# Adds moved behind their projections in VectorE's order, with three other placements, in a four-layer graph network kernel

## What is computed

```python
def L0(x, adj, w):                       # d = (rowsum(adj) + 1) ** -0.5
    return relu((d[:, None] * (adj + eye) * d[None, :]) @ x @ w)
def L1(x, adj, W, b):                    # s = (rowsum(adj) + 1e-8) ** -0.5
    return (s[:, None] * adj * s[None, :]) @ x @ W.T + b
def L2(x, A, W):                         # like L0, with rsqrt
    return relu(A_norm @ x @ W)
def L3(x, adj, ...):                     # attention and a plain aggregation, gated
    h = x @ W_sa
    e = where(adj != 0, exp(-leaky_relu(s_left[:, None] + s_right[None, :], 0.01)), 0)
    x_a = (e / (rowsum(e) + 1e-5)) @ h
    x_b = adj @ (x @ W_gcnb) + b_gcnb
    return sigmoid(attn_a * x_a + attn_b * x_b)
```

## Time and profile before

| | |
|---|---|
| median of 3 runs | 1775.53 us (1772.66 to 1776.35) |
| profiled execution | 1777.48 us, span 1775.7 us |
| TensorE busy | 1701.0 us, 96% of the span |
| VectorE, ScalarE, GpSimd busy | 63%, 44%, 34% |
| chunks by time | 6 begins at 399 us, 24 at 1392 us |

### The profile page before, as it was taken

How to read it: one execution, slowest core, us unless ns; L and a number is a source line. 1 busy time by engine, 2 the same in 40 slices (tenths; PEclk the granted TensorE clock), 3 DMA queues, 4 the chain that set the end, 5 groups by cost and what they waited for, 6 DMA issues and landing times.

```text
span 1775.7 us, 31699 instructions
## 1 busy us (share of the span) xinstructions
PE 1701.0 (96%) x12862; PEld 1164.4 (66%) x12862; DVE 1111.8 (63%) x1957; ACT 773.8 (44%) x1178; POOL 605.2 (34%) x567
## 2 busy tenths in 40 slices
PE   3999999999899998999999999999999999999998
PEld 1444444657786887887887887788788544444445
DVE  5786887967768666533543445553641566787765
ACT  5674655544444443322322223210111568677655
POOL 0001655537646444420321111121200446455441
PEclk9999999999999999999999999999999999999999
DMA  9994688698777879876664879976644443444434
GB/s 392 349 347 149 216 321 314 222 342 288 279 276 270 315 248 329 306 282 215 232 227 139 287 243 316 355 245 233 216 143 161 143 128 99 143 138 116 142 96 133
DMA packets 185559, 417.08 MB, mean 235 GB/s; under 512 B 18340, under 2 KB 79136, under 8 KB 181680
## 3 DMA queue, kind: packets, MB, share of 16 engines
q1 hardware_dynamic: 151544, 337.14, 56.4%
q10 hardware_dynamic: 33868, 77.90, 11.5%
HBM read 303.80 MB, written 111.17 MB: 234 GB/s over the span
## 4 chain that ended last, share of the span: by engine, by line
PE 74%; DVE 12%; DMA 5%; ACT 4%; POOL 2%; issue 2%; SPq 0%; ACTq 0%; DVEq 0%; POOLq 0%
PE ps L1139 15%; PE ps L1185 11%; PE ps L1186 11%; PE ps L1187 11%; PE ps L1232 7%; PE ps L1234 7%; PE ps L1233 7%; DVE U L1484 4%; DMA U<-in_adjT 3%; DVE stage L1467 1%; ACT U L1812 1%; DVE CT L1523 1%; DMA U<-in_adj 1%; ACT U L1735 1%; DVE OT L1530 1%
## 5 line engine op out<-in xcount | busy, mean ns | idle before, releaser
L1185 PE MATMUL ps<-U,HB 128*128 128x256 f16 (+2 forms) x2520 | 634.6, 260 | 8.6 <-DVE U L1484 4.1
L1186 PE MATMUL ps<-U,HB 128*128 128x256 f16 (+2 forms) x2520 | 634.4, 260 | 0.0
L1187 PE MATMUL ps<-U,HB 128*128 128x256 f16 (+2 forms) x2520 | 634.2, 260 | 0.0
L1232 PE MATMUL ps<-U,HB 128*128 128x512 f16 (+3 forms) x960 | 341.5, 359 | 21.4 <-DVE U L1484 14.4
L1233 PE MATMUL ps<-U,HB 128*128 128x512 f16 (+3 forms) x960 | 341.1, 358 | 0.0
L1234 PE MATMUL ps<-U,HB 128*128 128x512 f16 (+3 forms) x960 | 340.7, 358 | 0.0
L1484 DVE SCALAR_TENSOR_TENSOR U<-U,cS 128x512 f16<-128x512 f32 (+6 forms) x255 | 253.8, 1019 | 105.0 <-ACT U L1812 104.1
L1139 PE MATMUL ps<-W,OT 128*128 128x512 f16 (+1 forms) x1320 | 302.9, 384 | 9.9 <-DVE xr L1553 7.5
L1185 PEld LDWEIGHTS ps<-U,HB 128*128 128x128 f16 x2520 | 246.3, 98 | 38.8 <-DVE U L1484 5.2
L1812 ACT ACTIVATE U<-U,cS 128x512 f16<-128x512 f32 (+6 forms) x255 | 198.6, 803 | 159.3 <-POOL U L2006 49.7
L1186 PEld LDWEIGHTS ps<-U,HB 128*128 128x128 f16 x2520 | 246.5, 98 | 26.1
(11 more groups left out here) (207 smaller groups left out, 1884.3 us busy)
## 6 DMA issues: line engine op xcount, KB each, us to landing
U<-Ad SPq DMA_DIRECT2D x83, 896.0 KB, 6.7
U<-in_adjT SPq DMA_DIRECT2D x289, 256.0 KB, 4.4
Ad<-U ACTq DMA_DIRECT2D x35, 896.0 KB, 5.3
xd<-xr SPq DMA_DIRECT2D x84, 256.0 KB, 5.8
xr<-xd SPq DMA_DIRECT2D x84, 256.0 KB, 5.2
U<-in_adj SPq DMA_DIRECT2D x14, 1354.0 KB, 8.7
U<-Ad SPq DMA_DIRECT2D x23, 707.0 KB, 5.0
HBd<-stage ACTq DMA_DIRECT2D x16, 896.0 KB, 9.5
```

Source lines behind the costliest of these rows:

```text
L1185: eng.matmul(o, h[0], hi, start=J == 0 and a == 0, stop=False)
L1186: eng.matmul(o, h[0], lo, start=False, stop=False)
L1187: last = eng.matmul(o, h[1], hi, start=False, stop=to in "acg" and J == 9 and a == 1)
L1232: eng.matmul(o, h[0], hi, start=j == 0, stop=False)
```

## The change

Six edits to the planner; no stage is added or taken out but the merged ones.

1. `post(v, p, t)` in `spaced`: the post of a tile in chunks 6 to 23 stands right behind its `project`, no longer at `max(v + 1, later(v, 1.5))`.
2. `at_us` of chunk 6: layer 0's last four projections are planned at 6.5, 9.5, 12.5, 15.5 us instead of 8, 11.5, 15, 18.5.
3. `FETCH`: the first five adjacency rows of chunk 24 are fetched ahead of rows 18 to 21 of chunk 23. The old loop went by SEQ.
4. `pairs`: in layer 1, for J = 0 and 1, and for J = 2 and 3, spread, root and norms are done once for four tiles, when the second pair is complete.
5. `quiet` behind pair 9 is 6.5 us instead of 8; in layer 1 `xbias` and `x_keep` of pairs 9 and 10 are planned 4 us later.
6. `z_keep` stands 8 us behind its `post` instead of 5.2.

```diff
+_cut = AT["agg", GE - 1, 18]
+FETCH = SEQ[:_cut] + SEQ[_cut + 4:_cut + 9] + SEQ[_cut:_cut + 4] + SEQ[_cut + 9:]
...
-        while fetched < len(SEQ) and (fetched <= u + 9 or near(SEQ[fetched], u, 9, 28 if SEQ[fetched][1] == 12 else 20)):
-            g, j = SEQ[fetched][1:]
+        while fetched < len(SEQ) and (fetched <= u + 9 or near(FETCH[fetched], u, 9, 28 if FETCH[fetched][1] == 12 else 20)):
+            g, j = FETCH[fetched][1:]
...
+    def pairs(u, l, J):
+
+        both = l == 1 and J < 4
+        if both and J % 2 == 0:
+            return
+        J0 = J - 1 if both else J
+        t0, nt = 2 * J0, 2 * (J + 1 - J0)
+        put("spread", l, t0, nt)
+        late = 2.6 if l == 1 and J < 7 else 0
+        if late:
+            plan(max(later(u, late), u + 1), "root", l, t0, nt)
+        else:
+            put("root", l, t0, nt)
+        plan(max(later(u, 2.6 + late), u + 1), "norms", l, t0, nt)
+        for i in range(J0, J + 1):
+            pair(max(later(u, 5.2 + late), u + 2), l, i)
+
     def pair(u, l, J):
         nonlocal quiet
-        late = 2.6 if l == 1 and J < 7 else 0
-        if late:
-            plan(max(later(u, late), u + 1), "root", l, 2 * J, 2)
-        else:
-            put("root", l, 2 * J, 2)
-        plan(max(later(u, 2.6 + late), u + 1), "norms", l, 2 * J, 2)
-        u = max(later(u, 5.2 + late), u + 2, quiet)
+        u = max(u, quiet)
...
         if l == 1:
-            steps += [(5, "xbias", 2 * J), (5, "xbias", 2 * J + 1)]
-        steps += [(9, "x_keep", "post", l - 1, 2 * J), (9, "x_keep", "post", l - 1, 2 * J + 1)]
+            steps += [(5 if J < 9 else 9, "xbias", 2 * J), (5 if J < 9 else 9, "xbias", 2 * J + 1)]
+        steps += [(9 if l > 1 or J < 9 else 13, "x_keep", "post", l - 1, t) for t in (2 * J, 2 * J + 1)]
...
-        quiet = later(u, 8 if J >= 7 else 12)
+        quiet = later(u, 6.5 if J == 9 else 8 if J >= 7 else 12)
...
-            plan(later(v, 5.2), "z_keep", t)
+            plan(later(v, 8), "z_keep", t)
...
-        at_us = {0: (8, 11.5, 15, 18.5), 4: (9, 18), 5: (3, 10, 16.5, 23)}.get(c, (12, 18.5, 25, 31.5))
+        at_us = {0: (6.5, 9.5, 12.5, 15.5) if now == GW else (8, 11.5, 15, 18.5), 4: (9, 18), 5: (3, 10, 16.5, 23)}.get(c, (12, 18.5, 25, 31.5))
...
-            post(max(v + 1, later(v, 1.5)), p, t)
+            post(v, p, t)
...
             if stage[0] == "pair":
-                put("spread", stage[1], 2 * stage[2], 2)
-                pair(u, *stage[1:])
+                pairs(u, *stage[1:])
```

More of the change, by code:

```diff
@@ L344, in fetch_to @@
         while fetched < n:
-            put("fetch", *SEQ[fetched])
+            put("fetch", *FETCH[fetched])
             fetched += 1
```

## The result

The kernel after takes 1782.38 us (median; 1780.27 to 1783.36), the kernel before 1773.17 us in the same comparison: ratio 1.0033, 95% interval 1.0021 to 1.0045. It is slower by 0.33% (the two medians alone lie 0.52% apart; the ratio with its interval is used here). The forecast was 1756.6 us, and its range ended at 1769. The profiled execution of after took 1783.36 us with a span of 1781.5 us, 5.8 us more than before's 1775.7.

A forecast was written before the change was run, and what follows sets the result against it. TensorE was taken as the bound, busy 1701 of 1775.7 us. Gains of 4.0 (A), 8.9 (B), 6.0 (C) and 2 (D) sum to 20.9, less 2 is 18.9 us: 1756.6 us forecast, range 1747 to 1769.

The forecast's parts named there:

- B: Posts right behind projections, chunks 6 to 23: waits for the spare bank in chunks 8 to 11 go; gain 8.9 us.
- rival 2: Chunks 6 to 11: VectorE stands before the earlier adds, splits come late; 22 adds at 1.3 us, 1783 us; chance 0.07.
- C: Attention rows fetched earlier: masks start sooner, waits at chunk 24's first column and low clock go; gain 6.0 us.
- D: Layer 1, pairs 0 to 3, norms of four tiles at once: less VectorE work in chunks 2 and 3; gain 2 us.
- the 2 us taken off: Whole kernel: 2 us off the summed gain, because other waits grow when TensorE arrives earlier.
- rival 1: Chunks 7 to 12: released time returns as split or load waits, and D loses; gain 7.9, 1767.6 us; chance 0.19.
- A: Chunk 6, layer 0's last projections earlier: norms ahead of `lo`, waits for split and h shrink; gain 4.0 us.
- rival 4: Chunk 6: norms slowed once more beside GpSimd, 2.5 us less, gain 1.5 in A; 1759.1 us; chance 0.10.
- The clock term: Low clock behind most waits over 2 us: a removed wait also saves 1.65 to 3.4 us at the places priced.
- split waits of 480 to 740: Sign of being wrong: TensorE's waits for splits from 480 to 740 us exceed 3 us.
- full clock turned low at a new place: Sign of being wrong: a stretch at full clock turns low somewhere new; no size given.

The follow-up runs named there:

- only_post: The kernel before with the posts right behind their projections and `z_keep` at 8 us, alone: ratio 1.0025 to before.
- post_layer1: The kernel before with the early adds in layer 1 alone: ratio 0.9988 to before.
- only_c6: The kernel before with the new `at_us`, `quiet`, `xbias` and `x_keep` alone: ratio 0.9979 to before.
- only_fetch: The kernel before with the five attention rows fetched earlier, alone: ratio 0.9993 to before.
- after_post_layer1: The kernel after with the early adds kept in layer 1 alone: ratio 0.9970 to before.
- best_pairs: The kernel after with early adds in layer 1 alone and norms by two tiles as in before: ratio 0.9967 to before.
- post_vkeep16: As only_post, with the store of v's column (`v_keep`) planned two tiles of TensorE's order later: ratio 1.0018 to before.
- after_c6_old_post: The kernel after with the adds of chunk 6 alone one place later, as in before: ratio 0.9996 to before.
- best_acc: As after_post_layer1, with the place of the attention's two partial sums (acc) entered as two places: ratio 0.9952, 1769.27 against 1777.36 us for before.

## Why the prediction was wrong

**B failed, in the sentence on the layers that it does not gain in:** "In layers 2 and 3 TensorE waits for none of these adds: nothing." (Layer 0's adds in chunk 6 were not priced either.) TensorE did not wait for these adds, but VectorE and ScalarE now wait in front of them, and I counted only splits as queued behind, by TensorE's waits for them in layer 1. In chunk 6 the queue held two `normed` and splits, with the spread, `hi`, `lo` and the norms behind them; in chunk 18 it held `hi`, `lo`, `w_max`, `v_dot`, a store and a load. Cost: 2.9 to 5.6 us in chunk 6 (5.6 in after, 133.39 against 127.74), 4.5 to 5.6 us behind 982. This is rival 2's mechanism, but not at its price and only half in its place (chunks 6 to 11): not 22 adds at 1.3 us, but two places at 3 to 6 us each. That rival 2's 1783 us is within 1 us of the result is luck, for it set 28.6 us lost against 20.9 gained.

**The miss by terms.** The gain forecast was 18.9 us, the traces have a loss of 5.8, 24.7 us apart. Chunk 6 has 7.2 of them (+4.0 forecast, -3.2 measured; 5.6 is the price of the early adds), layer 1 has 11.4 (+8.9; +2.7 up to 721 and -5.2 behind), layer 2 has 5.6, C has 2.4, D 1.0; the 2 us taken off and the last 0.9 go the other way. So the unpriced waits in front of the adds are 11.2 us of the miss, and the gain of layer 1 that did not last is another 11.4.

**B's gain was about the right size up to 721, and did not last.** The waits for the bank went, in after from 7.5 to 0.2 us; from 462 to 721 only_post and post_layer1 had gained 7.7 and 6.3 us against the 8.9 forecast. In after only 2.7 us are left, since waits of 0.5 to 2.6 us for splits and one load came in chunks 8, 9 and 11: I had charged 2 us for splits, and TensorE's waits for them rose by 3.9. Then the 5.2 us behind 721 take the rest too (in post_layer1 only 0.7). That is rival 1, to which I had given 0.19 and a place in layer 1; why the time goes back behind 721 stays open.

**A was right alone in its first step, and undone in company.** In only_c6 the wait for the split is 1.58 us, 1.2 forecast, and full clock stands behind it. The wait for h of the last tiles, forecast at 1, grew from 1.85 to 2.15 us, and now the low clock stands behind that one:

```profile
458.00:464.00 6.00, 5.64 (x37) 4.44 (x38) 2.62 (x5) 0.00 (x0) 0.00 (x0) 0.72 0.97 384
```

This loss lies behind the mark at 462, so of the 2.5 us gained up to there 0.7 are left at 721 (388.3 against 389.0); 4.0 were forecast, bounds 1.85 and 6.2. The norms do stand ahead of `lo` in after, but slowed, as rival 4 feared. Two lines of VectorE there, in one chain of seven:

```profile
444.89 0.16 DVE L1448 RECIPROCAL RD<-RD 128x2 f32<-128x2 f32 x1
...
447.80 1.19 DVE L1457 SCALAR_TENSOR_TENSOR NB<-mv,SC 128x2 f32<-128x2 f32 x1
```

The 1.19 us lie beside GpSimd's addition of 1.27 us at 447.71. The Trainium skill ("SBUF — State Buffer", "Who interferes with whom") has it that a VectorE instruction with two SBUF inputs contends with a GpSimd instruction that reads SBUF, and the trace agrees. In only_c6 the chain of pair 10 is slowed alike (its last line takes 1.20 us), and it gained 2.5 us all the same; the lateness of 5.6 us in after came from the relus and the slowed chain of pair 9.

**C's step was right up to the last wait.** Counted from the mark early in chunk 22, the five loads were issued some 10 us earlier and the masks began 7 us earlier in after. I did not look at what the fourth mask waits for: GpSimd's first sum and its buffer. So 3.0 us of waits became 2.4, not 0, and the stretch took 430.1 to 431.8 us with the edit against 430.7 to 433.7 without: about 1 us. The clock, priced at 3.4 us, is not the edit's alone: behind the first column it is full in after, but 0.83 in only_fetch, after_post_layer1 and best_pairs with the same two waits, and full in post_vkeep16, which has the old loads and waits of 2.18 and 0.82 us. Before, at 0.66, was the lowest of all. With that buffer freed the stretch took 427.4, 6.3 less than before, against 6.0 forecast; against the other kernels without the edit it is 3.3 to 5.0, so the agreement is in part luck.

**D** was forecast at 2 us with bounds on both sides of nothing. Alone it gave 0.9995, and nothing up to 332 us (333.1 against 332.1). **`z_keep`, `x_keep`** and the take-off of 2 us show nowhere apart.

**The clock term** was added to each wait as if it were tied to it. The traces do not bear this out, as the last section shows: the same wait has the low clock behind it in one kernel and not in the next.

Of "what would show it", the split waits of 480 to 740 came out as the sign of failure named there (4.2 us against 3), and so did the full clock turned low at a new place.

## What to carry to other kernels

When an instruction is moved forward on an in-order engine, list all that is queued behind it up to the next wait of the bound engine, on this engine and on each that waits for it, and end the list at a transfer: the price is the longest wait in front of the moved instruction wherever that list has no lead. Move it only where the trace shows that someone waits for it; here taking the move back everywhere but in layer 1 turned +0.33% into -0.30%. And a removed wait is a gain only if the next late thing has room: here, in the mean of the traces, half of what layer 1 won up to 721 us was lost by 749, and in after all of it. And when a stall is to go by an earlier start, read every wait of the instructions that start early: a buffer's name may cover two buffers.

## What the runs showed of the hardware that I had not expected

**A small store in front of a load.** A store of 4 KB, written in pieces of 4 bytes, can hold a queue for longer than a load of 256 KB: issued behind the load in post_vkeep16, the store took 11.8 us to land, and the load 6.2. Windows of only_post around it:

```profile
1100.00:1105.00 5.00, 5.00 (x48) 4.48 (x47) 1.95 (x6) 3.43 (x3) 3.27 (x4) 1.00 1.26 215
1105.00:1110.00 5.00, 5.00 (x48) 4.47 (x47) 3.69 (x10) 1.31 (x3) 0.00 (x0) 1.00 0.84 39
```

And its DMA issues from 1103.5 us on (KB each, us from issue to landing):

```profile
U<-Ad SPq DMA_DIRECT2D x1, 256.0 KB, 17.1
```

The DMA engines are busy to 0.84 while they move 39 GB/s, and the load issued 2 us behind the store lands after 17.1 us. Weights of 1024 KB and two stores of x of 256 KB are issued between the two, within 1.6 us ahead of the load; in post_vkeep16 they are 2 to 4 us ahead of it, so not all of the 11 us between the loads need be the small store's. The Trainium skill ("DMA: Bandwidth & Descriptors", "Queues, rings and completion order") says that on each DMA engine the descriptors of a queue are consumed in ring order, which agrees with the store going first.

**The clock behind the same wait.** The low clock came behind each wait of 2.7 us at 747 and not behind those of 1.1 and 1.8 us at the same place. But elsewhere a wait of one length has either. At the end of chunk 6 the clock is 0.72 behind before's wait of 2.69 us, and full behind only_fetch's of 2.61 us at the same matmul:

```profile
453.00:459.00 6.00, 4.76 (x42) 4.03 (x42) 5.42 (x6) 5.54 (x9) 4.33 (x4) 1.00 0.96 291
```

only_fetch then waits 3.54 us for h instead of 1.85, and the low clock comes there. At that matmul for h only_c6, after_c6_old_post and best_acc have 0.72 behind 2.15 us, after_post_layer1 and best_pairs 1.00. At chunk 24's first column, waits of 2.18 us are followed by 0.66, 0.83 and 1.00. So the loss of 1.7 us can move from one side of a mark to the other without an edit at that place, and a forecast should give it a chance, not a certainty.
